# A third buffer in SBUF for the decays and states of a selective scan, and the shared bias as two rows of a low-rank product

## The chip, the cores and the metric

The kernel runs on one core of one Trainium2 chip. The metric is the device time of one execution in microseconds (us). TensorE is PE in the rows, VectorE is DVE, ScalarE is ACT, GpSimd is POOL, SyncE is SP.

## The reference, cut to what matters

The input is one sequence of 4096 tokens with 512 channels, float32. A layer norm is followed by a selective scan with 16 states per channel, its output is normed and added; then comes a mixture of 8 experts (top 2, 2048 hidden units, a low-rank side path of rank 32) and a shared expert that every token passes:

```python
dt = softplus(x_low @ W_dt + b_dt); A = -exp(A_log)
h  = exp(dt * A) * h + (dt * x) * B_t          # one state of 16, for every channel
y  = sum_n(h_n * C_t[n]) + x * D_skip
...
sh = gelu(xt @ sw1 + sb1) @ sw2 + sb2
sh = sh + gelu(xt @ swd) @ swu
out = out + 0.2 * sh
```

## The kernel before, in words

There are three stages, one after the other: `prepare` (norm, projections, step sizes), `mix` (the recurrence, with the shared expert of the first 7 of 8 blocks of 512 tokens laid between), and `experts` (the last shared block and the experts). The change is in `mix`.

`mix` walks over units g = 0 to 511, then on to 575 without a recurrence. A unit is one state n (16) of one group of 128 channels (4) of one chunk of 512 tokens (8), so 64 units make a chunk. Each engine has its own loop over g, and its instructions run in that written order; semaphores tie the engines together. For unit g:

- GpSimd (`drive`, L897) multiplies `dtx` by the row of B into `u`, a ring of 6, up to 5 units ahead. It may write `u` of unit g only when the scan of unit g - 6 is done. Both inputs lie in SBUF.
- ScalarE (`decay`, L646) writes exp(dt * A) into a buffer `bank(g)`. Before that it copies the last column of the unit that had the buffer (`keep`, L635) and so waits for that unit's product.
- VectorE (`recur`, L790) scans in place: bank = bank * previous + u. Then (`weigh`, L797) it multiplies bank by the row of C into `pr`, a ring of 5.
- TensorE (`add`, L1014) adds `pr` into PSUM by four transposing matmuls.

PSUM has eight banks. The shared expert needs four for its sums (`psS`), one for `psH`, and `psY` takes one, so `bank(g)` has two PSUM banks (`psA`). Up to unit 116 (`WIDE` = 117) the first `psS` bank is still free and serves as a third. With three, VectorE is told to do scan g + 1 and then product g; with two, it does scan g and product g in turn, and ScalarE is two units ahead instead of three.

The shared expert of block b sits at hand-written unit numbers from the start of chunk b + 1: `UP_AT` the first products (L1050), `BURST_AT` the gelus on ScalarE, `HI_AT` and `LO_AT` the split of the hidden values in a high and a low part (L715 on ScalarE, L906 on GpSimd, which reads SBUF only), `DOWN_AT` the second products (L1061, L1071). GpSimd also issues the loads of its weights (L950, L959), each when a slot is free. At unit 119 of a block (`OUT_AT`) VectorE takes the four `psS` banks out, times 0.2 plus the bias 0.2 * sb2 that a 128 x 512 tile `b2bc` holds (`shared_out`, L841). `low_rank_lo` (L828) forms the low part of the low-rank hidden values, from two SBUF tiles into one. `static_lo` (L847 to L853) prepares the low-rank weights once, at unit 10.

## Time and profile before

| what | value |
|---|---|
| median of 3 runs | 3389.76 us (3389.55 to 3391.35) |
| span of the profiled execution, first to last instruction | 3388.4 us |
| `prepare` in the trace | 0 to about 150 us |
| units 0 to 116, three buffers | about 152 to 393 us |
| units 117 to 511, two buffers | about 393 to 1306 us |
| rest of the last shared block | 1306 to about 1387 us |
| `experts` | about 1387 us to the end |

No time is given for the profiled execution apart from its span; the span is 1.4 us short of the median of the runs, which is what lies around it. Times in the trace count from the first instruction. "Busy" is the time in which an engine carries out an instruction; idle time stands beside it with what ended it.

### The profile page before, as it was taken

How to read it: one execution, taken by the hardware profiler on the slowest of the kernel's cores; microseconds unless marked ns; L12 is line 12 of the kernel's file. 1: busy time of each engine (PE TensorE's matmuls, PEld its weight loads, DVE VectorE, ACT ScalarE, POOL GpSimd, SP SyncE). 2: the span in 40 equal slices, each digit the busy share in tenths (PEclk: the TensorE clock that was granted, in tenths of full speed). 3: DMA queues.
4: the chain of work that ended last, by engine and by line, in shares of the span. 5: the costliest groups of instructions: out<-in, count | busy, mean ns of one | idle time of the engine just before them, and what ended most of it. 6: DMA issues, size and time to landing. Idle time of an engine off the chain costs nothing.

```text
span 3388.4 us, 42962 instructions
## 1 busy us (share of the span) xinstructions
PE 3100.0 (91%) x15139; PEld 2538.6 (75%) x15139; DVE 1812.1 (53%) x2476; ACT 1633.6 (48%) x2978; POOL 1384.2 (41%) x1367
## 2 busy tenths in 40 slices
PE   6464799988989899999999999999999999999997
PEld 3243677777767777788888888888888888888886
DVE  7797989988998984441331332322313313313345
ACT  7654676666767665452332432433423424324343
POOL 2297787988988785311110121021111111211224
PEclk9655899999999999999999999999999999999999
DMA  7968678696977865930320420412312303204355
GB/s 265 303 189 250 163 229 217 203 268 183 257 192 225 230 190 186 288 95 19 88 69 13 106 60 16 119 37 54 97 20 75 78 16 100 63 10 115 75 184 161
DMA packets 273447, 466.30 MB, mean 138 GB/s; under 512 B 30817, under 2 KB 102193, under 8 KB 273234
## 3 DMA queue, kind: packets, MB, share of 16 engines
q1 hardware_dynamic: 200400, 264.91, 26.5%
q0 software_dynamic: 66720, 189.87, 21.3%
q10 hardware_dynamic: 6114, 8.79, 0.7%
q8 instruction: 121, 1.98, 0.2%
q14 instruction: 92, 0.75, 0.1%
HBM read 366.33 MB, written 97.16 MB: 137 GB/s over the span
## 4 chain that ended last, share of the span: by engine, by line
PE 53%; DMA 2%; DVE 2%; issue 1%; ACT 1%; POOL 0%; SPq 0%; POOLq 0%; DVEq 0%; ACTq 0%
PE c_psH L2030 26%; PE c_psY L2071 25%; PE c_psT L2021 1%; DMA out<-d_y 1%; PE c_psY L2067 0%; DVE yst L1734 0%; DMA raw<-in_w 0%; DMA W2l<-ws_d 0%; DVE hl L1754 0%; ACT h L1487 0%; DVE hl L1759 0%; DVE wgt L1923 0%; PE c_psT L2130 0%; DVE hh L1753 0%; DMA d_x1p<-x_d 0%
## 5 line engine op out<-in xcount | busy, mean ns | idle before, releaser
L1759 DVE TENSOR_TENSOR hl<-h,hh 128x512 fp32r<-128x512 f32 (+1 forms) x400 | 242.5, 606 | 1185.3 <-ACT hh L1491 1185.2
L1489 ACT ACTIVATE h<-c_psH,biases 128x512 f32<-128x512 f32 (+1 forms) x400 | 248.1, 620 | 1045.0 <-PE c_psH L2030 1033.0
L897 POOL TENSOR_TENSOR u<-dtxs,Bt 128x512 f32<-128x512 f32 x512 | 669.3, 1348 | 148.2 <-DVE b_psA L790 132.9
L790 DVE TENSOR_TENSOR_SCAN b_psA<-b_psA,b_few,u 128x512 f32<-128x512 f32 x473 | 606.4, 1282 | 75.0 <-ACT b_psA L646 74.0
L2071 PE MATMUL c_psY<-W2h,hh 128*128 128x512 f32 x1344 | 535.2, 398 | 1.8 <-DVE hl L1759 1.1
L1014 PE MATMUL b_psY<-ident,pr 128*128 128x128 f32 x2048 | 345.7, 308 | 208.2 <-DVE pr L797 190.1
L2071 PE MATMUL c_psY<-W2l,hh 128*128 128x512 f32 x1344 | 525.4, 391 | 0.0
L2071 PE MATMUL c_psY<-W2h,hl 128*128 128x512 f32 x1344 | 524.4, 390 | 0.0
L1567 POOL DMA_INDIRECT xrow<-xt_d,slot_lists x80 | 84.7, 1059 | 1050.3 <-PE c_psT L2021 600.2
L1014 PEld LDWEIGHTS b_psY<-ident,pr 128*128 128x128 f32 x2048 | 265.9, 156 | 290.8 <-DVE pr L797 238.7
L646 ACT ACTIVATE b_psA<-dts,wgt 128x512 f32<-128x512 f32 x473 | 327.4, 692 | 14.9 <-ACT b_few L635 0.2
L797 DVE TENSOR_TENSOR pr<-b_psA,Ct 128x512 f32<-128x512 f32 x473 | 325.5, 688 | 14.4 <-DMA Ct<-bc_d 0.7
L1050 PE MATMUL b_psH<-Xh,w 128*128 128x512 f32 x896 | 316.7, 415 | 9.9 <-DMA w<-ws_d 9.7
L1607 POOL DMA_INDIRECT acc_d<-yst,slot_lists x72 | 117.4, 1630 | 442.7 <-DVE yst L1734 425.3
L2071 PEld LDWEIGHTS c_psY<-W2h,hl 128*128 128x128 f32 x1344 | 252.8, 188 | 54.9
L2071 PEld LDWEIGHTS c_psY<-W2h,hh 128*128 128x128 f32 x1344 | 253.2, 188 | 53.2 <-DVE hl L1759 6.2
L1071 PE MATMUL b_psS<-w,hhs 128*128 128x512 f32 x896 | 292.7, 408 | 0.0
L2071 PEld LDWEIGHTS c_psY<-W2l,hh 128*128 128x128 f32 x1344 | 253.5, 189 | 46.6 <-issue 0.2
L1491 ACT ACTIVATE hh<-c_psH,biases 128x512 fp32r<-128x512 f32 (+1 forms) x400 | 245.1, 613 | 0.0
L2030 PE MATMUL c_psH<-Xh,W1h 128*128 128x512 f32 x576 | 224.5, 390 | 0.7 <-DMA W2l<-ws_d 0.7
L2030 PE MATMUL c_psH<-Xl,W1h 128*128 128x512 f32 x576 | 224.3, 389 | 0.0
L2030 PE MATMUL c_psH<-Xh,W1l 128*128 128x512 f32 x576 | 224.2, 389 | 0.0
(271 smaller groups left out, 5685.1 us busy)
## 6 DMA issues: line engine op xcount, KB each, us to landing
w<-ws_d POOLq DMA_DIRECT2D x224, 512.0 KB, 6.6
raw<-in_w SPq DMA_DIRECT2D x256, 256.0 KB, 2.8
Bt<-bc_d SPq DMA_DIRECT2D x64, 512.0 KB, 14.6
Ct<-bc_d SPq DMA_DIRECT2D x64, 512.0 KB, 19.1
xn<-in_x SPq DMA_DIRECT2D x8, 1024.0 KB, 7.9
xT_d<-xnT SPq DMA_DIRECT2D x8, 1024.0 KB, 12.5
dt_d<-a_dt SPq DMA_DIRECT2D x8, 1024.0 KB, 8.5
dtx_d<-a_dx SPq DMA_DIRECT2D x8, 1024.0 KB, 8.7
```

What stands on the lines that cost most here:

```text
L646: nc.scalar.activation(bank(g)[:, :], dts[s % 2][:, :], ACT.Exp, scale=A_neg[:, s % DT, n:n + 1]).then_inc(s_dA, 1)
L790: nc.vector.tensor_tensor_scan(a[:, :], a[:, :], u[g % U_RING][:, :], carry[:, k:k + 1], ALU.mult, ALU.add).then_inc(s_h, 1)
L797: nc.vector.tensor_tensor(pr[g % PR_RING][:, :], bank(g)[:, :], C_of(g), ALU.mult)\
L897: nc.gpsimd.tensor_tensor(u[g % U_RING][:, :], dtx[s % 2][:, :], Bt[n // TG][:, n % TG, :], ALU.mult)\
L1014: last = nc.tensor.matmul(psY[:, t, :], pr[g % PR_RING][:, t * P:(t + 1) * P], ident[:, :], start=(n == 0 and t == 0), stop=False, is_tran ...
L1050: last = nc.tensor.matmul(out, a[:, d, :], v[:, d, :], start=(d == 0 and i == 0), stop=(d == DT - 1 and i == 2))
L1071: last = nc.tensor.matmul(psS[t][:, :], a, v, start=False, stop=(j == FC and i == 2))
L1489: nc.scalar.activation(h32[:, 0:n * P], psH[j % 2][:, 0:n * P], ACT.Gelu, bias=b1[:, j - 1:j])
L1491: nc.scalar.activation(hh[j % 2][:, 0:n * P], psH[j % 2][:, 0:n * P], ACT.Gelu, bias=b1[:, j - 1:j]).then_inc(s_gelu, 1)
L1759: nc.vector.tensor_tensor(hl[j % 2][a], h32[a], hh[j % 2][a].bitcast(F32), ALU.subtract)\
L2030: last = nc.tensor.matmul(out, a, b, start=(i == 0), stop=(i == n - 1))
L2071: last = nc.tensor.matmul(psY[t][:, :], a[j % 2][:, c], b, start=False, stop=(j == J - 1 and i == 2))
```

## The change: what it does, and the diff

From unit 117 on, every third unit (g % 3 = 2) uses `decay_aside`, a 128 x 512 tile in SBUF, as its `bank`; the others use the two `psA` banks in turn. So there are three buffers throughout, ScalarE is three units ahead in all units, and VectorE does scan g + 1 before product g in all units. Units 0 to 116 keep their three PSUM banks.

The tile `b2bc` and its load go. `sb2` comes as two rows below the low-rank weights `L2`, which grow from 96 to 98 rows; the rows hold the high and the low part of sb2, and `hh0` gets two rows of ones against them. `static_lo` makes these rows by three more VectorE instructions of 2 x 512. `shared_out` becomes a plain multiplication by 0.2 on ScalarE, one bank at each of units 119 to 122.

```diff
-        g0, hh0 = sb("g0", [P, CH]), sb("b_low_h", [L3, CH], F32R)
-        b2bc = sb("sb2bc", [P, D])
+        aside = sb("decay_aside", [P, CH])
+        g0, hh0 = sb("g0", [P, CH]), sb("b_low_h", [L3B, CH], F32R)
         yst = two("ysh", [P, D]) + xn
...
         def bank(g):
 
-            if g < WIDE:
-                return (psA + psS[0:1])[g % 3]
-            return psA[(g - WIDE) % 2]
+            if g % 3 < 2:
+                return psA[g % 3]
+            return psS[0] if g < WIDE else aside
...
                 sp.dma_start(wu_raw[k * LR:(k + 1) * LR, :], w["swu"]).then_inc(s_stat, 16)
+            sp.dma_start(wu_raw[L3:L3B, :], w["sb2"].partition_broadcast(2)).then_inc(s_stat, 16)
             for i in range(4):
                 load_raw(i)
-            sp.dma_start(b2bc[:, :], w["sb2"].partition_broadcast(P)).then_inc(s_bias, 16)
...
                     for t in range(BT):
-                        if due(b, OUT_AT) + 1 + t == g:
+                        if due(b, OUT_AT + t) + 1 == g:
                             store_sh(b, t)
...
             def decay(g):
-                s, n, old = g // NS, g % NS, g - (3 if g < WIDE + 2 else 2)
+                s, n, old = g // NS, g % NS, g - 3
                 if n == 0:
                     loaded(act, s)
-                if g == WIDE + 2:
-                    keep(old - 1)
                 if old >= 0:
                     keep(old)
                     act.wait_ge(s_cd, old + 1)
...
-                nc.scalar.copy(hh0[:, :], g0[0:L3, :]).then_inc(s_h0a, 1)
+                nc.scalar.copy(hh0[0:L3, :], g0[0:L3, :]).then_inc(s_h0a, 1)
...
+            def shared_out(b, t):
+                if b < FB - 1:
+                    act.wait_ge(s_mm2, (b + 1) * J)
+                else:
+                    act.wait_ge(s_tile, t + 1)
+                after(act, s_sh[t], b * 16)
+                if t >= 2:
+                    act.wait_ge(s_T, min(b + 2, FB + 1) * BT)
+                    act.wait_ge(s_xt[t - 2], min(b + 2, FB + 1) * (BT // 2) * 16)
+                nc.scalar.mul(yst[t][:, :], psS[t][:, :], SHARE).then_inc(s_yev, 1)
...
-                if g + 3 < WIDE + 2:
+                if g + 3 < UNITS:
                     decay(g + 3)
-                elif WIDE + 2 <= g + 2 < UNITS:
-                    decay(g + 2)
                 if g == 6:
                     static_hi()
-                if g == NU:
-                    act.wait_ge(s_bias, 32)
-                    nc.scalar.mul(b2bc[:, :], b2bc[:, :], SHARE).then_inc(s_b02, 1)
...
+                    for t in range(BT):
+                        if due(b, OUT_AT + t) == g:
+                            shared_out(b, t)
...
+            nc.vector.memset(hh0[L3:L3B, :].bitcast(F32), 1.0).then_inc(s_one, 1)
...
-            def shared_out(b, t):
-                if b < FB - 1:
-                    dve.wait_ge(s_mm2, (b + 1) * J)
-                else:
-                    dve.wait_ge(s_tile, t + 1)
-                dve.wait_ge(s_b02, 1)
-                after(dve, s_sh[t], b * 16)
-                if t >= 2:
-                    dve.wait_ge(s_T, min(b + 2, FB + 1) * BT)
-                    dve.wait_ge(s_xt[t - 2], min(b + 2, FB + 1) * (BT // 2) * 16)
-                nc.vector.scalar_tensor_tensor(yst[t][:, :], psS[t][:, :], SHARE, b2bc[:, :], ALU.mult, ALU.add)\
-                    .then_inc(s_yev, 1)
-
             def static_lo():
-                dve.wait_ge(s_stat, 5 * 16)
+                dve.wait_ge(s_stat, 6 * 16)
...
+                two_rows = slice(L3, L3B)
+                nc.vector.tensor_tensor(bias_low, wu_raw[two_rows, :], L2[two_rows, :].bitcast(F32),
+                                        ALU.subtract).then_inc(s_blow, 1)
+                dve.wait_ge(s_blow, 1)
+                nc.vector.tensor_scalar(bias_low, bias_low, ident[two_rows, L3 + 1:L3 + 2], None, ALU.mult)\
+                    .then_inc(s_blow, 1)
+                dve.wait_ge(s_blow, 2)
+                nc.vector.scalar_tensor_tensor(L2[two_rows, :], L2[two_rows, :].bitcast(F32), ident[two_rows, L3:L3 + 1],
+                                               bias_low, ALU.mult, ALU.add).then_inc(s_l2, 1)
...
-                if g <= WIDE:
-                    if g == 0:
-                        recur(0)
+                if g == 0:
+                    recur(0)
+                if g + 1 < UNITS:
                     recur(g + 1)
-                    weigh(g)
-                elif g < UNITS:
-                    if g > WIDE + 1:
-                        recur(g)
+                if g < UNITS:
                     weigh(g)
 
...
+                    pe.wait_ge(s_one, 1)
                     for t in range(BT):
-                        last = nc.tensor.matmul(psS[t][:, :], hh0[:, t * P:(t + 1) * P], L2[:, :], start=True, stop=False)
+                        last = nc.tensor.matmul(psS[t][:, :], hh0[0:L3B, t * P:(t + 1) * P], L2[0:L3B, :],
+                                                start=True, stop=False)
                 else:
```

## Rows read from the trace of the kernel before

**Rows 1.** Chain that ended last, share of the span, by engine.

```profile
PE 53%; DMA 2%; DVE 2%; issue 1%; ACT 1%; POOL 0%; SPq 0%; POOLq 0%; DVEq 0%; ACTq 0%
```

**Rows 2.** Busy time in stretches: length, engines' busy us (instructions), clock, DMA share, GB/s.

```profile
393.00:1306.00 913.00, 818.57 (x4329) 677.03 (x4328) 822.93 (x943) 618.56 (x1155) 763.96 (x746) 0.96 0.77 217
1306.00:1387.00 81.00, 76.66 (x347) 62.30 (x345) 11.66 (x25) 28.32 (x36) 37.65 (x65) 0.98 0.64 200
1387.00:3388.40 2001.40, 1975.89 (x9625) 1654.45 (x9625) 650.00 (x1141) 746.79 (x1397) 353.09 (x359) 1.00 0.30 80
```

**Rows 3.** VectorE's groups by line, 393 to 1306 us: busy, mean ns | idle before.

```profile
L790 DVE TENSOR_TENSOR_SCAN b_psA<-b_psA,b_few,u 128x512 f32<-128x512 f32 x395 | 506.9, 1283 | 54.8 <-ACT b_psA L646 53.8 <-POOL u L897 0.5
L797 DVE TENSOR_TENSOR pr<-b_psA,Ct 128x512 f32<-128x512 f32 x396 | 273.9, 692 | 13.6
L822 DVE TENSOR_TENSOR Xl<-b_psH,Xh 128x512 fp32r<-128x512 f32 x24 | 16.5, 686 | 17.0 <-ACT Xh L676 17.0
L812 DVE BATCH_NORM_STATS2 b_few<-ys 128x6 f32<-128x512 f32 x24 | 15.2, 682 | 3.5 <-DMA ys<-in_x 3.5
L802 DVE BATCH_NORM_STATS2 b_few<-ys 128x6 f32<-128x512 f32 x24 | 14.8, 680 | 0.1
L828 DVE TENSOR_TENSOR b_low_h<-g,b_low_h 32x512 fp32r<-32x512 f32 x7 | 8.1, 1154 | 0.2
L841 DVE SCALAR_TENSOR_TENSOR ysh<-b_psS,sb2bc 128x512 f32<-128x512 f32 x12 | 7.7, 681 | 0.0
```

**Rows 4.** VectorE's timeline in the two-buffer stretch: start us, length us, what.

```profile
801.46 1.28 DVE L790 TENSOR_TENSOR_SCAN b_psA<-b_psA,b_few,u 128x512 f32<-128x512 f32 x1
802.78 0.69 DVE L797 TENSOR_TENSOR pr<-b_psA,Ct 128x512 f32<-128x512 f32 x1
803.38 1.28 DVE L790 TENSOR_TENSOR_SCAN b_psA<-b_psA,b_few,u 128x512 f32<-128x512 f32 x1
```

**Rows 5.** VectorE's timeline in the three-buffer stretch.

```profile
167.90 1.28 DVE L790 TENSOR_TENSOR_SCAN b_psS<-b_psS,b_few,u 128x512 f32<-128x512 f32 x1
169.09 0.67 DVE L797 TENSOR_TENSOR pr<-b_psA,Ct 128x512 f32<-128x512 f32 x1
169.68 1.28 DVE L790 TENSOR_TENSOR_SCAN b_psA<-b_psA,b_few,u 128x512 f32<-128x512 f32 x1
```

**Rows 6.** ScalarE's groups by line, 393 to 1306 us.

```profile
L646 ACT ACTIVATE b_psA<-dts,wgt 128x512 f32<-128x512 f32 x394 | 272.8, 692 | 12.3
L635 ACT COPY b_few<-b_psA 128x1 f32<-128x1 f32 x394 | 61.2, 155 | 177.1 <-DVE pr L797 173.8
L676 ACT CAST Xh<-b_psH 128x512 fp32r<-128x512 f32 x24 | 14.0, 584 | 7.7 <-PE b_psH L1033 7.7
```

**Rows 7.** VectorE's groups by shape, whole span: instructions with only SBUF operands.

```profile
L1756 DVE TENSOR_TENSOR hh<-h,hl 32x512 fp32r<-32x512 f32 x17 | 11.6, 683 | 0.6
...
L853 DVE TENSOR_TENSOR L<-ys,L 32x512 fp32r<-32x512 f32 x1 | 1.7, 1685 | 0.0
...
L1830 DVE TENSOR_TENSOR_SCAN RA<-xrow,RB 128x512 f32<-128x512 f32 x1 | 1.2, 1225 | 0.0
```

**Rows 8.** VectorE's timeline around the last low-rank split.

```profile
1291.48 1.28 DVE L790 TENSOR_TENSOR_SCAN b_psA<-b_psA,b_few,u 128x512 f32<-128x512 f32 x1
...
1293.53 1.16 DVE L828 TENSOR_TENSOR b_low_h<-g,b_low_h 32x512 fp32r<-32x512 f32 x1
```

**Rows 9.** GpSimd's timeline over the same time.

```profile
1292.85 1.29 POOL L897 TENSOR_TENSOR u<-dtxs,Bt 128x512 f32<-128x512 f32 x1 [0.64 <-DVE b_psA L790]
1294.10 1.72 POOL L906 TENSOR_TENSOR hls<-hb,hhs 128x512 fp32r<-128x512 f32 x1
```

**Rows 10.** GpSimd's groups by line, 393 to 1306 us.

```profile
L897 POOL TENSOR_TENSOR u<-dtxs,Bt 128x512 f32<-128x512 f32 x390 | 514.0, 1351 | 135.2 <-DVE b_psA L790 124.0 <-DMA dtxs<-dtx_d 2.9 <-DVE b_psS L790 0.4
L906 POOL TENSOR_TENSOR hls<-hb,hhs 128x512 fp32r<-128x512 f32 x100 | 134.5, 1345 | 1.1 <-ACT hhs L715 1.0
...
L959 POOL DMA_DIRECT2D w<-ws_d x96 | 65.4, 681 | 0.0
```

More of the change, by code:

```diff
@@ L367 @@
 L3 = 3 * LR
+L3B = L3 + 2
 T_AT, X_HI_AT, X_LO_AT = (24, 27, 31, 34), (25, 29, 32, 35), (27, 31, 34, 37)
@@ L447, in mix @@
         s_sh = [sem(f"b_sh_stored{t}") for t in range(BT)]
-        s_bias, s_b02 = sem("b_biases_in"), sem("b_bias_scaled")
+        s_bias, s_blow, s_one = sem("b_biases_in"), sem("b_bias_low"), sem("b_bias_rows_of_ones")
         s_wr = [sem(f"b_raw_w_in{k}") for k in range(4)]
@@ L456, in mix @@
         gate_raw = ys[1][:, 1, 0:DT * E].rearrange("p (a n) -> p a n", a=DT)
-        wu_raw = ys[1][0:L3, 2, :]
+        wu_raw = ys[1][0:L3B, 2, :]
+        bias_low = ys[1][L3:L3B, 3, :]
         def raw_pair(i):
@@ L689, in hidden_out @@
                     act.wait_ge(s_wl, FC)
-                    act.wait_ge(s_bias, 32)
+                    act.wait_ge(s_bias, 16)
                 nc.scalar.activation(hb[:, n % HB_RING, :], psH[:, :], ACT.Identity,
@@ L731, in static_hi @@
             def static_hi():
-                act.wait_ge(s_stat, 5 * 16)
+                act.wait_ge(s_stat, 6 * 16)
                 nc.scalar.copy(L1h[:, :, 0:L3].rearrange("p a (g n) -> p a g n", g=3),
@@ L864, in _ @@
                 for b in blocks(g):
-                    if due(b, OUT_AT) == g:
-                        for t in range(BT):
-                            shared_out(b, t)
                     if due(b, LOW_LO_AT) == g:
@@ L1039, in up @@
                     pe.wait_ge(s_llo, 2)
-                    pe.wait_ge(s_l2, 1)
+                    pe.wait_ge(s_l2, 2)
                     wh, wl = L1h, L1l
@@ L1308, in piece @@
                 a = slice((w_ - 2) * 256, (w_ - 1) * 256)
-                return WU[:, a], r[0:L3, 0:256], L2[:, a], L2[0:LR, a], r[0:L3, 0:256]
+                return WU[:, a], r[0:L3, 0:256], L2[0:L3, a], L2[0:LR, a], r[0:L3, 0:256]
             j = (w_ - 4) // 2
@@ L2066, in down @@
                                 pe.wait_ge(s_yev, at["t0"] - (2 if at["k"] == 1 else 4) + min(t, 1 if at["k"] == 1 else 3) + 1)
-                            last = nc.tensor.matmul(psY[t][:, :], hh[0][0:L3, c], L2[:, :], start=True, stop=False)
+                            last = nc.tensor.matmul(psY[t][:, :], hh[0][0:L3, c], L2[0:L3, :], start=True, stop=False)
                             continue
@@ L2215, in program @@
             kept_tile("edge2", [P, 8], F32)
-            const["L2"] = kept_tile("L2", [L3, D])
+            const["L2"] = kept_tile("L2", [L3B, D])
             const["X"] = [kept_tile(f"X{h}", [P, DT, CH]) for h in "hl"]
```

1 line of the change is left out of this document (removed).

## The prediction

> **What bounds the kernel now.** I read the chain first, for where a saving could count [rows 1]: TensorE holds 53% of it, VectorE 2%. That sum is over stages with different limits, so I cut the span into stages [rows 2]. From 1306 us on TensorE is busy 95 to 99% of the time, and the change touches nothing there but the four last reads of PSUM. What it touches is the stretch of units 117 to 511, 913 us long. There TensorE is busy 818.6 us and VectorE 822.9 us, and GpSimd 764.0 us. The next view says what VectorE does with its time [rows 3]: 395 scans and products, and beside them the parts of the shared expert, the statistics, and the waits in front.
>
> The pace of a unit comes from the timeline. With two buffers scan follows scan after 803.38 - 801.46 = 1.92 us [rows 4]; with three, where the next scan stands between a scan and its product, after 169.68 - 167.90 = 1.78 us [rows 5]. The difference is that the product starts 1.32 us after its scan in the one and 1.19 us after the scan before it in the other.
>
> The 913 us of VectorE then add up: 395 x 1.92 = 758; waits for ScalarE's decays 54; the split of X 16.5 + 17.0 of wait; statistics 15.2 + 3.5 + 14.8 and about 5 of their short second halves, in smaller groups; low-rank split 8; taking out the shared sums 24 x 0.64 = 15 (12 of them stand in the row, 12 more cost the same) [rows 3]. That is 908, so VectorE's queue sets the pace here, the product of each unit feeds TensorE, and what is left of TensorE's time, 913 - 819 = 94 us, is the room below it. When the recurrence is over, 81 us of TensorE work remain whatever came before [rows 2]: a shift of the recurrence shifts the end by the same amount, as long as TensorE is not itself the bound.
>
> **What the change takes away.** (a) The pace: 395 x (1.92 - 1.78) = 55 us. (b) The waits for decays, 53.8 us [rows 3]. They come when ScalarE's gelus stand ahead of a decay. ScalarE will be three units ahead instead of two, one unit more is 1.78 us, and ScalarE waited 174 us for products over the stretch [rows 6], so it has the time. I let 10 us stay: -44. (c) `shared_out` leaves VectorE: -15. On ScalarE it costs 24 x 0.58 = 14 us by the copy of a bank of the same size [rows 6], in the same 174 us of waiting; without that cover it would come back as 14 us of decays. In the ScalarE queue the decay of three units ahead stands behind each of the four, at one per unit, and the last second product is due 7 units ahead of them, so no new wait for TensorE is likely. At the end of the last block four takings on one engine replace four on the other: 0. The scaling of `b2bc` and its load go, off the path: 0. Two more rows in four matmuls a block cost 0, since the rows are contracted in parallel, and their columns stay.
>
> VectorE's sum without anything else would be 913 - 55 - 44 - 15 = 799 us, and TensorE's 819 would stop it first.
>
> **What the change adds: operands in SBUF on an engine that shares.** Units 119 to 509 in steps of 3 are 131. Their scan reads `aside` and `u`, both in SBUF; their product reads `aside` and the row of C, both in SBUF. Before, one operand was always in PSUM. Alone this costs nothing: a scan of this size with SBUF operands took 1225 ns and a 512-wide product 683 ns, both with GpSimd idle [rows 7]; the decay's write to SBUF instead of PSUM I put at 0, inside ScalarE's slack.
>
> With GpSimd at work it is another matter. `low_rank_lo` is the one repeated instruction of this stage with two SBUF inputs, and it takes 1154 ns [rows 3] where the same shape takes 683 in the last stage [rows 7]. Its neighbours show why. It starts at 1293.53 while GpSimd's `u` runs until 1292.85 + 1.29 = 1294.14, and it ends at 1294.69, 0.55 us behind that [rows 8, 9]. GpSimd's next instruction starts at 1294.10 and takes 1.72 us instead of 1.29, so it ends at 1295.82, 1.13 us behind VectorE's end: it too waited. Each works only when the other has finished. Once-run L853 was 1685 ns in the same way [rows 7]. The product is delayed here by 0.47 us, GpSimd by 0.44 us (1.72 - 1.28). No scan with two SBUF inputs next to a busy GpSimd is in the trace. I take it to behave as this product does, bounded below by 0 (no collision) and above by a whole GpSimd instruction, 1.29 us.
>
> On VectorE: `u` starts 0.09 us after the end of the scan that frees it (1291.48 + 1.28 = 1292.76, then 1292.85) [rows 8, 9]. It ends 1.38 us after that scan. The next scan comes 1.78 - 1.28 = 0.50 us after it, so a scan into `aside` waits 0.88 us, less the 0.14 that a waiting instruction has saved of its start (0.69 - 0.55): 0.74 us. The product into `pr` comes 1.19 us after the start of the scan ahead of it, before that scan's end has released `u`; it waits nothing where GpSimd is caught up, and about 0.47 where GpSimd is in arrears. I take 0.25. That gives 131 x 0.74 = 97 and 131 x 0.25 = 33, and VectorE's sum is 799 + 130 = 929 us.
>
> On GpSimd: a product holds it up 0.44 us; a scan takes 0.53 us longer to stream (1225 against 683 ns), so 0.97. Where GpSimd is only issuing DMAs it reads nothing; the share of its time in `u` and the low parts is (514.0 + 134.5) / 764 = 85% [rows 2, 10]. Its sum is 764 + 131 x 1.41 x 0.85 = 921 us.
>
> So two engines that had slack toward each other come to 929 and 921, and GpSimd's work is uneven. Between units 59 and 105 of a block stand 16 low parts, 16 weight loads of one kind and about 14 of the other: (16 x 1.25 + 30 x 0.68) / 46 x 3 = 2.6 us per three units, with 3 x 1.25 for `u` and 1.2 for the collisions 7.6 us, or 2.5 us a unit; VectorE's own is 929 / 395 = 2.35. With 46 of 64 units at 2.5 and 18 at 2.35 the stretch would be 971 us. The five units that GpSimd may be ahead smooth part of that. I take the middle of 929 and 971: 950 us, +37 us.
>
> The Trainium skill, SBUF — State Buffer, section "Who interferes with whom", states that a VectorE instruction with two SBUF inputs and a GpSimd instruction that reads SBUF exclude each other for the whole instruction, whoever came first. With whole instructions (1.28 + 0.69) in place of the trace's 1.41 GpSimd's sum would be 764 + 131 x 1.97 x 0.85 = 983 us instead of 921; the trace agrees with the exclusion and not quite with its length, since 0.44 us was lost for a 0.69 us instruction.
>
> (d) Three more VectorE instructions in `static_lo`, in the early stretch where its queue is tight: two with two SBUF inputs like L853, at most 1.69 each [rows 7], one with a single input, about 0.5, each behind a wait on the one before: between 2 and 4, I take +4 us.
>
> Sum: +37 + 4 = +41 us. Against the profiled span 3388.4 that is 3429.4; the median of the runs lies 1.4 above the span: 3431 us.
>
> **The rivals.** *It gets faster: scans don't collide.* The trace shows the collision for products only. If a scan in SBUF runs beside GpSimd, VectorE comes to 799 + 33 = 832 and GpSimd to 764 + 131 x 0.44 x 0.85 = 813, TensorE's 819 is next to them, and with as much unevenness as above (+21) the stretch takes about 853: 3390 - 60 + 4 = 3334 us. The place is the 131 scans alone; it turns at the price per scan at which VectorE's sum plus 21 is 913, (913 - 853) / 131 = 0.46 us. For it speaks that a scan takes 1.28 us for 512 columns, over twice a product's streaming, so it asks for operands at half the rate; against it, that what was seen was no sharing of a rate but a wait until the other had ended.
>
> *It gets much slower: the arrears chain.* A low part that comes late holds TensorE's second product, which stands in the same queue as the sums of `pr`; the ring of 5 fills, and ScalarE's next split waits for TensorE. Then every product waits 0.47, VectorE's sum is 799 + 131 x 1.21 = 958, and the two kinds of wait for ScalarE (54 + 17, of which 10 + 17 were kept) come back with 44, to 1002: 3390 + 89 + 4 = 3483 us. For it speaks that ScalarE and TensorE already wait on one another here; against it, the 94 us of room in TensorE.
>
> *It does nothing.* Gains of 114 us (55 + 44 + 15) against 114 us of collisions: that needs 0.87 us per unit into `aside`, between the two prices above, 3390 us. Nothing favours this point, it only lies on the way.
>
> **How the numbers follow.** My forecast's case (both collide, 3395 to 3465) 0.50; the chain (above 3465) 0.17; the faster case (below 3383) 0.26, some of it with part of the collision; within the band of no change 0.07. A measurement of this kernel tells a change from none at about 0.2%, 7 us. The range goes from 3334 to 3485, the rival's time on either side; a tenth may lie beyond each end. The likeliest case alone: 3402 (products free, no unevenness beyond GpSimd's 921) to 3465.
>
> **What would show it.** In the changed profile the scans into `aside` should last 1.8 to 2.2 us instead of 1.28 and their products up to 1.2; GpSimd's `u` should have a longer mean than 1351 ns and wait less for scans than 124 us; the waits of L790 for ScalarE should fall from 54 to about 10; scans into `psA` should keep their 1.28. The stretch from unit 117 to 511 should take 950 us. Scans into `aside` at 1.23 to 1.3 us would make the forecast wrong and the faster rival right. TensorE waiting for low parts (L906), which it does not now, would point to the chain.

## The result, and the profile after

| | before | after |
|---|---|---|
| median of 4 runs each on one chip | 3390.56 us | 3518.50 us (3516.77 to 3523.50) |
| span of the profiled execution | 3388.4 us | 3516.7 us |
| units 117 to 511 | 393 to 1306 us, 913 us | 393 to 1434 us, 1041 us |
| what remains of the last shared block | 81 us | 82 us |

The ratio is 1.0377 (1.0365 to 1.0390): 128 us slower. The direction was forecast (3431 us), the size was not: 3518 lies above the end of the range, 3485. All of the difference is in the stretch of units 117 to 511, 1041 - 913 = 128 us, where 950 us stood in the forecast. That is read from the stretches of the kernel after (columns as in [rows 2]):

```profile
393.00:1434.00 1041.00, 855.49 (x4350) 691.99 (x4349) 1000.51 (x924) 640.45 (x1185) 825.89 (x751) 0.94 0.69 192
1434.00:1516.00 82.00, 77.76 (x352) 63.14 (x350) 8.57 (x20) 31.47 (x43) 38.52 (x67) 0.98 0.65 202
```

VectorE was busy 822.9 us there before [rows 2] and is busy 1000.5 of 1041 us now: it is the bound, with hardly a gap. GpSimd, which the forecast had at 921 us, is at 826. VectorE's groups over that stretch, kernel after (busy us, mean ns | idle before), against [rows 3]:

```profile
L800 DVE TENSOR_TENSOR_SCAN b_psA<-b_psA,b_few,u 128x512 f32<-128x512 f32 x266 | 339.5, 1276 | 17.9 <-ACT b_psA L646 17.6
L800 DVE TENSOR_TENSOR_SCAN decay_aside<-decay_aside,b_few,u 128x512 f32<-128x512 f32 x131 | 286.4, 2186 | 12.9 <-ACT decay_aside L646 11.0 <-ACT b_few L637 1.8
L807 DVE TENSOR_TENSOR pr<-decay_aside,Ct 128x512 f32<-128x512 f32 x131 | 199.7, 1524 | 0.1
L807 DVE TENSOR_TENSOR pr<-b_psA,Ct 128x512 f32<-128x512 f32 x266 | 176.5, 664 | 0.1
L832 DVE TENSOR_TENSOR Xl<-b_psH,Xh 128x512 fp32r<-128x512 f32 x24 | 16.3, 677 | 6.3 <-ACT Xh L676 6.3
```

Two kinds of row stand next to each other here, one in PSUM and one in SBUF, and only the second has changed. Scans into `psA` keep their 1276 ns; scans into `decay_aside` take 2186, so 131 x 0.910 = 119 us more. Products from `psA` take 664 ns; those from `decay_aside` take 1524, so 131 x 0.860 = 113 us more. These are 232 us in place of the 130 forecast. Waits for decays are 17.6 + 11.0 + 1.8 = 30.4 us (53.8 before, 10 forecast). With 397 x 1.78 = 707 us for the units, 22.6 for the split of X, about 35 for the statistics and 10 for the low-rank split the sum is 707 + 232 + 30 + 23 + 35 + 10 = 1037 of 1041 us. The rows account for the whole stretch.

The means hide how the collisions are distributed. The tile's own view of the kernel after gives shortest, median and longest, in ns:

```profile
L800 DVE TENSOR_TENSOR_SCAN decay_aside<-decay_aside,b_few,u x131: 1253/1943/4872, 401.2 to 1425.9; 128x512 f32<-128x512 f32 x131
L807 DVE TENSOR_TENSOR pr<-decay_aside,Ct x131: 662/674/5229, 407.6 to 1428.9; 128x512 f32<-128x512 f32 x131
```

Half of the products pass unhindered (674 ns), and yet their mean is 1524: the sum is in a tail of up to 5.2 us, four times a GpSimd instruction. Over all 131 units, 30 products and 27 scans lost more than 1.3 us each, a whole GpSimd instruction; these 57 waits hold 151 of the 232 us (about 91 in the products and 60 in the scans). The other 101 products lost 0.22 us on average, the other 104 scans 0.57. One of the long waits in VectorE's timeline, kernel after, with the three added instructions of `static_lo` above it:

```profile
177.39 1.64 DVE L853 TENSOR_TENSOR ys<-ys,L 2x512 f32<-2x512 f32 x1
179.07 0.48 DVE L856 TENSOR_SCALAR ys<-ys,ident 2x512 f32<-2x512 f32 x1
179.59 0.75 DVE L859 SCALAR_TENSOR_TENSOR L<-L,ident,ys 2x512 fp32r<-2x512 f32 x1
...
802.69 1.28 DVE L800 TENSOR_TENSOR_SCAN b_psA<-b_psA,b_few,u 128x512 f32<-128x512 f32 x1
803.88 4.83 DVE L807 TENSOR_TENSOR pr<-decay_aside,Ct 128x512 f32<-128x512 f32 x1
808.64 1.28 DVE L800 TENSOR_TENSOR_SCAN b_psA<-b_psA,b_few,u 128x512 f32<-128x512 f32 x1
```

And GpSimd over the same time, kernel after:

```profile
803.20 0.58 POOL L950 DMA_DIRECT2D w<-ws_d  x1
803.79 1.31 POOL L897 TENSOR_TENSOR u<-dtxs,Bt 128x512 f32<-128x512 f32 x1
805.06 1.29 POOL L906 TENSOR_TENSOR hls<-hb,hhs 128x512 fp32r<-128x512 f32 x1
806.29 0.57 POOL L959 DMA_DIRECT2D w<-ws_d  x1
806.88 1.27 POOL L897 TENSOR_TENSOR u<-dtxs,Bt 128x512 f32<-128x512 f32 x1
```

The product should have waited for the `u` of 803.79 and then had its turn. It waited through three reading instructions and a DMA issue, and ended at 803.88 + 4.83 = 808.71, 0.56 us behind the end of the last (806.88 + 1.27 = 808.15). GpSimd's instructions meanwhile kept their 1.3 us: it did not give way once. 0.56 us is what a product had left to run in [rows 8, 9] too (0.55), so the end of a wait looked as forecast, and its length did not.

### The profile page after: what moved, and what is told of

The parts are those of the page before. It is cut to its first block, busy times and chain, and to the rows that moved or that the text cites. A ratio compares the mean times of both kernels' runs of the same rounds, so it can differ in the third digit from the quotient of the medians.

```text
span 3516.7 us, 42960 instructions
## 1 busy us (share of the span) xinstructions
PE 3134.1 (89%) x15139; PEld 2550.1 (73%) x15139; DVE 1985.6 (56%) x2452; ACT 1654.3 (47%) x3004; POOL 1443.0 (41%) x1367
## 4 chain that ended last, share of the span: by engine, by line
PE 51%; DVE 2%; DMA 2%; issue 1%; ACT 1%; SPq 0%; POOL 0%; POOLq 0%; DVEq 0%; ACTq 0%
PE c_psH L2032 25%; PE c_psY L2073 24%; PE c_psT L2023 1%; DMA out<-d_y 1%; DMA raw<-in_w 1%; PE c_psY L2069 0%; DVE yst L1736 0%; DVE hl L1756 0%; ACT h L1489 0%; DVE hl L1761 0%; PE c_psT L2132 0%; DVE hh L1755 0%; DMA d_x1p<-x_d 0%; DVE wgt L1925 0%; ACT h L1491 0%
## 5 line engine op out<-in xcount | busy, mean ns | idle before, releaser
L897 POOL TENSOR_TENSOR u<-dtxs,Bt 128x512 f32<-128x512 f32 x512 | 698.1, 1387 | 178.8 <-DVE b_psA L800 86.0
L1014 PE MATMUL b_psY<-ident,pr 128*128 128x128 f32 x2048 | 361.1, 312 | 312.9 <-DVE pr L807 287.7
L800 DVE TENSOR_TENSOR_SCAN b_psA<-b_psA,b_few,u 128x512 f32<-128x512 f32 x342 | 436.4, 1276 | 36.4 <-ACT b_psA L646 36.0
L1073 PE MATMUL b_psS<-w,hhs 128*128 128x512 f32 x896 | 303.4, 421 | 0.0
L800 DVE TENSOR_TENSOR_SCAN decay_aside<-decay_aside,b_few,u 128x512 f32<-128x512 f32 x131 | 286.4, 2186 | 12.9 <-ACT decay_aside L646 11.0
L646 ACT ACTIVATE b_psA<-dts,wgt 128x512 f32<-128x512 f32 x342 | 236.6, 692 | 10.9 <-ACT b_few L637 0.2
L807 DVE TENSOR_TENSOR pr<-b_psA,Ct 128x512 f32<-128x512 f32 x342 | 227.5, 665 | 0.6 <-DMA Ct<-bc_d 0.5
```

The source lines that it names most:

```text
L646: nc.scalar.activation(bank(g)[:, :], dts[s % 2][:, :], ACT.Exp, scale=A_neg[:, s % DT, n:n + 1]).then_inc(s_dA, 1)
L800: nc.vector.tensor_tensor_scan(a[:, :], a[:, :], u[g % U_RING][:, :], carry[:, k:k + 1], ALU.mult, ALU.add).then_inc(s_h, 1)
L807: nc.vector.tensor_tensor(pr[g % PR_RING][:, :], bank(g)[:, :], C_of(g), ALU.mult)\
L897: nc.gpsimd.tensor_tensor(u[g % U_RING][:, :], dtx[s % 2][:, :], Bt[n // TG][:, n % TG, :], ALU.mult)\
L1014: last = nc.tensor.matmul(psY[:, t, :], pr[g % PR_RING][:, t * P:(t + 1) * P], ident[:, :], start=(n == 0 and t == 0), stop=False, is_tran ...
L1073: last = nc.tensor.matmul(psS[t][:, :], a, v, start=False, stop=(j == FC and i == 2))
```

## The experiments

Times of the kernel before in the comparisons were 3390 to 3397 us; each ratio is against those of its own chip.

**The bias alone.** `shared_out` on ScalarE and the bias as rows, with the buffers and the order of the kernel before.

```diff
+TWO = 117
...
+            if g >= TWO:
+                return psA[(g - TWO) % 2]
```

> The bias as two rows and the taking out of the shared sums on ScalarE are kept; the buffers and the order of units are those of before (two PSUM banks from unit 117 on). If the whole loss comes from operands in SBUF, this part is a small gain: 24 takings x 0.64 = 15 us off VectorE, about 3 us lost in the static part: 3373 to 3380 us. If the takings on ScalarE delay decays and are part of the loss, it is slower than before: 3395 us or more.

3391.35 us, ratio 1.0005 (0.9994 to 1.0015): no change. The 15 us that left VectorE came back in front of its scans. The scans' row over 397 to 1316 us, kernel with the bias alone, against the 53.8 of [rows 3]:

```profile
L807 DVE TENSOR_TENSOR_SCAN b_psA<-b_psA,b_few,u 128x512 f32<-128x512 f32 x395 | 507.0, 1283 | 72.4 <-ACT b_psA L651 70.9 <-POOL u L907 1.0
```

**The SBUF buffer in half of the units.** `decay_aside` for units 117 to 314 (66 of them), two buffers after that, by the same edit with `TWO = 315` and the order of scans and products to match.

> The changed kernel with the SBUF buffer for units 117 to 314 alone (66 of its 131 units), two PSUM banks after that. If each unit in SBUF pays for itself, the time lies halfway between the bias part alone and the full change: about 3446 us. If the loss is an engine that falls into arrears over the whole stretch, the first half costs less than the second and the time is below 3420 us.

Ratio 1.0189 (1.0166 to 1.0211), some 3453 us, half of the way. The scans into `decay_aside` took 2146 ns and their products 1547, as in the whole. So the loss goes with the number of SBUF units, and the bias contributes nothing of its own. The order of scans and products changed together with the buffer, so this run does not tell the two apart.

**Turns by force.** GpSimd's `u` waits until the scan and the product of the SBUF unit are done, so that it can't run ahead of them.

```diff
+                if g - 5 > WIDE and (g - 5) % 3 == 2:
+                    pool.wait_ge(s_h, g - 5 + 1)
+                if g - 6 > WIDE and (g - 6) % 3 == 2:
+                    pool.wait_ge(s_pd, g - 6 + 1)
```

> The changed kernel with two more waits on GpSimd: around each unit in SBUF the next u starts only when that unit's scan is done, and the one after only when its product is done. GpSimd does the same work, with fewer chances to run on ahead. If VectorE's two-input instructions lose because GpSimd chains several instructions before it lets them in, this is faster than the changed kernel: 3430 to 3480 us. If GpSimd's own sum is what bounds the changed kernel, added waits on it make it slower: 3530 us or more.

3491.47 us, ratio 1.0301 (1.0282 to 1.0319): 27 us of the 128 came back. The products fell from 1524 to 1222 ns, the scans rose from 2186 to 2318. The time lies between the two that were expected. It helped part of the products, and gave no cause.

**The collision by itself.** A kernel that computes nothing of the reference: GpSimd runs a chain of six 128 x 512 products from SBUF, VectorE starts beside it a delay with an operand in PSUM and then one instruction under test.

> No part of the reference is computed. Twenty short cases one after the other: GpSimd runs six products of 128 x 512 from SBUF, without or with a wait that is already met before each, and VectorE issues one product or one scan at different offsets, with both inputs in SBUF, one in PSUM, or on 32 partitions. If the two take turns, VectorE's instruction lasts at most about 1.9 us (the rest of one GpSimd instruction and its own 0.55), a scan 2.4. If GpSimd keeps the port while it has work, VectorE's lasts to the end of the six: 5 to 7 us. With one input in PSUM 0.69 us in any case; alone 0.69 and 1.23.

VectorE's timeline of this kernel; L104 is the delay, L107 the product with one operand in PSUM, L109 the product with two in SBUF, L113 the scan with two in SBUF:

```profile
15.90 0.68 DVE L107 TENSOR_TENSOR do<-ps,db 128x512 f32<-128x512 f32 x1
23.07 0.43 DVE L104 TENSOR_TENSOR pre<-ps,da 128x256 f32<-128x256 f32 x1 [6.48 <-ACTq L86]
23.41 0.68 DVE L109 TENSOR_TENSOR do<-da,db 128x512 f32<-128x512 f32 x1
24.16 0.42 DVE L104 TENSOR_TENSOR pre<-ps,da 128x256 f32<-128x256 f32 x1
24.50 1.27 DVE L113 TENSOR_TENSOR_SCAN do<-da,few,db 128x512 f32<-128x512 f32 x1
25.85 0.23 DVE L104 TENSOR_TENSOR pre<-ps,da 128x64 f32<-128x64 f32 x1
25.99 1.72 DVE L109 TENSOR_TENSOR do<-da,db 128x512 f32<-128x512 f32 x1
...
66.00 2.04 DVE L113 TENSOR_TENSOR_SCAN do<-da,few,db 128x512 f32<-128x512 f32 x1
...
122.89 10.05 DVE L109 TENSOR_TENSOR do<-da,db 128x512 f32<-128x512 f32 x6
```

Beside GpSimd the product in PSUM takes its 0.68 us; with two operands in SBUF it is 0.68 without GpSimd and up to 1.72 with it, and a scan goes from 1.27 to 2.04: scans do collide, which ended the faster rival. But even six products in a row took turns with GpSimd, 10.05 us for six, 1.68 each. No wait here was longer than one GpSimd instruction. That left the tail without a cause.

**GpSimd that doesn't read.** From unit 117 on `u` is filled with a constant and not computed, in the kernel after and in the kernel before.

```diff
+                if g < WIDE:
                     nc.gpsimd.tensor_tensor(u[g % U_RING][:, :], dtx[s % 2][:, :], Bt[n // TG][:, n % TG, :], ALU.mult)\
                         .then_inc(s_u, 1)
+                else:
+                    nc.gpsimd.memset(u[g % U_RING][:, :], 0.5).then_inc(s_u, 1)
```

> The changed kernel, but from unit 117 on GpSimd fills u with a constant instead of multiplying two SBUF tiles into it: the product dt*x*B is left out there. GpSimd then reads SBUF only for the low parts (100 instructions in the stretch). If VectorE's two-input instructions wait for GpSimd's reads, scans into the SBUF buffer fall from 2.19 to about 1.4 us and their products from 1.52 to about 0.8, and the time falls to 3320 to 3360 us. If operands in SBUF are slow in themselves, or any GpSimd instruction collides, the scans stay near 2 us and the time above 3450 us.

> The kernel before with the same constant fill in place of dt*x*B from unit 117 on, as the measure for the run above. GpSimd does not set the pace there, so 3380 to 3392 us. If this one falls to 3350 us or less, GpSimd was part of the bound before the change, and my reading of that stretch was wrong.

The kernel after: 3377.26 us, ratio 0.9955 (0.9939 to 0.9971). The kernel before: 3381.31 us, 0.9970 (0.9959 to 0.9980). VectorE's groups, 397 to 1292 us, kernel after with the fill:

```profile
L800 DVE TENSOR_TENSOR_SCAN b_psA<-b_psA,b_few,u 128x512 f32<-128x512 f32 x264 | 338.0, 1280 | 59.7 <-ACT b_psA L646 59.2
L800 DVE TENSOR_TENSOR_SCAN decay_aside<-decay_aside,b_few,u 128x512 f32<-128x512 f32 x131 | 176.2, 1345 | 20.7 <-ACT decay_aside L646 19.7 <-ACT b_few L637 0.9
L807 DVE TENSOR_TENSOR pr<-b_psA,Ct 128x512 f32<-128x512 f32 x263 | 175.4, 667 | 0.1
L807 DVE TENSOR_TENSOR pr<-decay_aside,Ct 128x512 f32<-128x512 f32 x131 | 106.6, 814 | 0.1
```

Two things are seen. The scans are back at 1345 ns and the products at 814. A fill is also shorter than a product (549 ns on average), so the means alone could come from a GpSimd that has less to do. The single instructions settle it: of the 262 on the SBUF buffer 133 ran beside fills and not beside a reading instruction, and none of them was delayed; all 28 that were delayed by more than 0.1 us stood beside an instruction that reads. So the collision is with GpSimd's reads: it cost 3518 - 3377 = 141 us between these two kernels. The Trainium skill, SBUF — State Buffer, section "Who interferes with whom", states that a VectorE instruction with two SBUF inputs contends with a GpSimd instruction that reads SBUF and not with one that only writes it; 1345 against 2186 ns agrees. And without the collision the change is worth 3381 - 3377 = 4 us, hardly more than the runs scatter, not the 114 of the forecast: 59.2 + 19.7 = 79 us of waits for decays stand where 10 were expected.

**Where the 114 us went.** The same pair, with the third of the three products of each high and low pair left out (`up` and `down` with two instead of three), so that TensorE has less work.

```diff
-                    for i, (a, v) in enumerate(((wh, Xh), (wh, Xl), (wl, Xh))):
+                    for i, (a, v) in enumerate(((wh, Xh), (wh, Xl))):
...
-                        for i, (a, v) in enumerate(((hi, w2h), (hi, w2l), (lo, w2h))):
+                        for i, (a, v) in enumerate(((hi, w2h), (hi, w2l))):
```

> The changed kernel with the constant fill of u, and TensorE's work for the shared expert made lighter: of three products per pair of high and low parts the third is left out (L1050 and its sister), in the scan stage. Without collisions the change was worth only 4 us of 114. If that is because TensorE's queue, with ScalarE waiting behind it, bounds the stretch, this kernel falls well below 3377 us, to 3290 to 3330 us, and its VectorE waits 20 us or less for decays. If ScalarE's gelus alone hold the decays up, it stays above 3350 us.

> The kernel before with the same fill and the same lighter TensorE, the measure for the run above. VectorE's pace of 1.92 us a unit and its waits for gelus bound it then: 3350 to 3370 us, 30 us or more above its sister. If both fall together, the third buffer is worth nothing in any case.

After 3324.05 us, 0.9806 (0.9777 to 0.9834); before 3338.68 us, 0.9849 (0.9820 to 0.9877). The change is now worth 15 us instead of 4, less than expected. Lighter TensorE work took 53 us off the one and 43 off the other, so TensorE was part of the floor, and not all of it: 59 us of waits for decays stay, where 20 or less were expected. Waits for transfers come up as well: in the kernel after so lightened TensorE waits 23 us for weights (0.4 with the fill alone) and ScalarE 25 us for step sizes (3.6), over 393 to 1292 us. In the kernel after with the fill, ScalarE was then freed of its gelu tables by an identity in the gelu's place.

```diff
-                    nc.scalar.activation(hb[:, k:k + 2, :], hb[:, k:k + 2, :], ACT.Gelu).then_inc(s_g, 1)
+                    nc.scalar.activation(hb[:, k:k + 2, :], hb[:, k:k + 2, :], ACT.Identity).then_inc(s_g, 1)
```

> The changed kernel with the constant fill of u, and the gelus of the scan stage replaced by the identity, on the same engine: their values are left out, and with them the loads of the function tables, 50 x 1.28 us. If ScalarE's bursts are what keeps VectorE waiting, 3300 to 3335 us; if it is TensorE, not below 3355 us.

3351.28 us, 0.9886 (0.9857 to 0.9915): 26 us less, short of the 3335 us that were expected of ScalarE alone. Not all of it need be ScalarE's, since the granted clock of TensorE over 397 to 1240 us was 0.99 here and 0.96 with the fill alone. ScalarE and TensorE each seem to hold a part; how large each is stays open. In the trace of the kernel after with the fill, over the same 397 to 1292 us, ScalarE waits 66.7 us for TensorE's first products, and TensorE 73.4 us for VectorE's: the three wait in a ring, and shortening one of them moves the others little.

**Relative starts.** The collision by itself again, in 30 cases: a scan ahead of the product, a product ahead of the scan, and delays of 64 to 512 columns.

> No part of the reference is computed. GpSimd runs six products of 128 x 512 from SBUF in a row; VectorE issues one instruction with two SBUF inputs, in 15 steps of about 33 ns against GpSimd's chain: a product behind a scan from PSUM and ahead of another, and a scan between two products from PSUM, as in the changed kernel. If what VectorE runs ahead decides whether it gets its turn, some offsets show a product of 2.5 us and more (two or more GpSimd instructions passed). If they always take turns, all lie between 0.67 and 1.9 us (scans 1.25 to 2.4), and what lets GpSimd pass several times in the kernel is something else.

Products 1.28 to 1.74 us, scans 1.27 to 1.65. No start gave a wait beyond one GpSimd instruction.

**The SBUF buffer only where the gelus stand.** 25 units in place of 131: one ahead of each of the four bursts of a block, the rest on two PSUM banks.

```diff
+        in_sbuf = {(b + 1) * NU + at + 3 for b in range(FB) for at in BURSTS if (b + 1) * NU + at + 3 > WIDE}
...
+            return (psA + psS[0:1] + [aside])[keys[g]]
```

> The SBUF buffer is used for 25 units alone, each the third unit after the start of a burst of gelus on ScalarE, so that one more decay is ready there; all others use two PSUM banks, and the bias part is kept. Against the bias part alone (3391 us) it should take back most of VectorE's 70 us of waits for decays, -50, and pay 25 times the collisions that the changed kernel paid per unit (0.91 + 0.86 us), +44, less the pace of the units behind it, 50 x 0.14 = 7: 3370 to 3390 us. If a unit in SBUF costs more at these places, because GpSimd has its low parts to do right behind the bursts, 3400 us or more.

3423.71 us, ratio 1.0089 (1.0072 to 1.0106), so 32 us lost by 25 units, where 3370 to 3390 us had been expected. That is a miss, and it pointed to the cause. The tile's view and VectorE's timeline of this kernel:

```profile
L817 DVE TENSOR_TENSOR_SCAN decay_aside<-decay_aside,b_few,u x25: 1257/1260/10183, 400.5 to 1319.7; 128x512 f32<-128x512 f32 x25
```

```profile
764.41 8.72 DVE L817 TENSOR_TENSOR_SCAN decay_aside<-decay_aside,b_few,u 128x512 f32<-128x512 f32 x1 [0.78 <-ACT decay_aside L661]
```

GpSimd in the same time:

```profile
764.30 0.59 POOL L979 DMA_DIRECT2D w<-ws_d  x1
764.90 2.56 POOL L917 TENSOR_TENSOR u<-dtxs,Bt 128x512 f32<-128x512 f32 x2
767.40 1.30 POOL L926 TENSOR_TENSOR hls<-hb,hhs 128x512 fp32r<-128x512 f32 x1
768.64 0.58 POOL L970 DMA_DIRECT2D w<-ws_d  x1
769.23 1.27 POOL L917 TENSOR_TENSOR u<-dtxs,Bt 128x512 f32<-128x512 f32 x1
770.46 1.26 POOL L926 TENSOR_TENSOR hls<-hb,hhs 128x512 fp32r<-128x512 f32 x1
771.67 0.58 POOL L979 DMA_DIRECT2D w<-ws_d  x1
```

One scan of 8.72 us let five reading instructions pass, and it had asked just when a weight load was being issued (764.30); the product of 803.88 above had asked right behind such an issue (803.20). The trace of the kernel after says the same when its delayed scans and products are sorted by what GpSimd was at when they asked, with more of its work to follow without a gap:

| GpSimd at the request | delayed | passed by a further reading instruction |
|---|---|---|
| at a DMA issue, or right behind one | 57 | 50 |
| an issue two or four instructions back | 31 | 7 |
| no issue since GpSimd's last gap | 56 | 0 |

In 30 of the 31 an instruction of an SBUF unit had been served since the issue. In a few cases it is open whether they belong in the first row or the second.

The table holds delayed requests alone, and that hides half of the first row. 42 requests fell into an issue itself, while GpSimd read nothing. 27 of them went at once, 15 were delayed, and 13 of these let a reading instruction pass. Of the 39 that fell into the first reading instruction behind an issue, or came as it started, with more behind it, every one was delayed and 35 let a further one pass. So an issue does not always shut VectorE out; what the 27 had in their favour is not known.

How the waits ended can be read too. The 57 that let a further reading instruction pass ended 34 times with GpSimd's queue empty and 23 times while GpSimd was at a later DMA issue, never with a reading instruction directly behind. The product of 540.56 us took 3.00 us in this way: it let two `u` pass and had its turn when the issue of 542.95 began.

**Other suspects.** The collision by itself in 28 cases: semaphore waits on VectorE, waits on GpSimd, a scan in place, and a DMA issue after the second product of the chain, which is later than VectorE's request.

> No part of the reference is computed. Seven kinds of case at four offsets each, with GpSimd running six products from SBUF: a plain product behind a scan from PSUM; with met waits in front of it; with a DMA issue in GpSimd's chain; a scan in place; waits on both sides; GpSimd waiting for VectorE's semaphore; and all together. If one of these lets GpSimd pass several times, that kind shows a VectorE instruction of 2.5 us and more. If none does, all products stay below 1.9 and scans below 2.4 us, and the cause lies in something of the full kernel that these leave out.

Products 1.28 to 1.75 us, scans 1.81 to 2.27. All took turns; waits and the in-place form are not the cause, and neither is an issue that comes after the request.

**The weight loads issued elsewhere.** The loads of L950 and L959, 112 of each, in the kernel after and in the kernel before are issued by SyncE, with the same waits and the same places in the order of units (the tile is taken as plain float32 there). The 192 of the two expectations is too low: in units 117 to 511 of the kernel after stand 198 of the 224:

```profile
L950 POOL DMA_DIRECT2D w<-ws_d x101 | 64.4, 638 | 12.3 <-PE b_psH L1050 10.9 <-issue 1.4
L959 POOL DMA_DIRECT2D w<-ws_d x97 | 64.3, 663 | 3.6 <-PE b_psS L1073 3.2 <-issue 0.4
```

```diff
-                nc.gpsimd.dma_start(w1[k][:, :, :, :].rearrange("p h a f -> p (h a f)"),
+                sp.dma_start(w1[k][:, :, :, :].rearrange("p h a f -> p (h a f)").bitcast(F32),
```

> The changed kernel with the 192 loads of the shared expert's weights issued by SyncE at the same unit numbers instead of GpSimd. GpSimd's queue gets shorter by 129 us of issues in the stretch and its products stand less often in arrears. If VectorE's long waits (2.5 us and more) come of a GpSimd that has several instructions due at once, they get fewer and the time falls by 30 to 60 us, to 3460 to 3490 us. If a DMA issue in GpSimd's chain is itself what shuts VectorE out, they vanish altogether and it falls by 80 us or more. If neither, 3510 to 3525 us.

> The kernel before with the same loads issued by SyncE, the measure for the run above. GpSimd had slack there, so the loads alone should change nothing: 3385 to 3395 us. If SyncE's queue holds the loads behind its other waits, TensorE waits for weights and it is slower.

After 3446.49 us, 1.0163 (1.0146 to 1.0180); before 3435.77 us, 1.0129 (1.0112 to 1.0146). VectorE's groups, 393 to 1434 us, kernel after with the loads on SyncE:

```profile
L829 DVE TENSOR_TENSOR_SCAN decay_aside<-decay_aside,b_few,u 128x512 f32<-128x512 f32 x131 | 238.7, 1822 | 21.9 <-ACT decay_aside L675 20.8 <-ACT b_few L666 0.8
...
L836 DVE TENSOR_TENSOR pr<-decay_aside,Ct 128x512 f32<-128x512 f32 x131 | 147.6, 1127 | 0.1
```

The waits over 1.3 us fall from 57 to 8, and what they hold from 151 to 28 us. GpSimd still issues the loads of `x` (L951, 16 of them), and all 8 long waits asked at or behind one of these.

A rival is left: without the issues GpSimd might simply have less in arrears, so that less stands ready to pass. The trace says no. 113 delayed requests met a GpSimd that had more to follow without a gap and had issued nothing since its last gap, twice the 56 of the kernel after, and none was passed by a further instruction.

The change now costs 3446 - 3436 = 11 us and not 128. The 11 us is not the price of the short collisions: scans and products on the SBUF buffer still take 71 + 61 = 132 us more than as many in PSUM (1822 against 1278 ns, 1127 against 665), and the kernel before lost 46 us by the move. SyncE is no gain by itself: TensorE waits 45.0 us for weights in the kernel before with the loads there (9.7 without the move), and VectorE 98.2 us for decays (53.8).

**The issue ahead of the request.** The collision by itself in 28 cases, with one DMA issue ahead of the first, second or third of GpSimd's six products, and VectorE's request after 1, 3, 5 or 7 delays of 0.6 us.

```diff
+                    if what != "none" and j == at:
+                        nc.gpsimd.dma_start(px[:, :], a["x"][0:P, :]).then_inc(s_x, 16)
                     nc.gpsimd.tensor_tensor(po[j][:, :], pa[:, :], pb[:, :], ALU.mult).then_inc(s_p, 1)
```

> No part of the reference is computed. In the changed kernel 50 of 57 requests of VectorE that met a GpSimd instruction directly behind a DMA issue, or the issue itself, with more of GpSimd's work behind, were passed by at least one more; of 93 others 7 were. So here GpSimd runs six products from SBUF with one DMA issue ahead of the first, second or third, and VectorE asks with two SBUF inputs after 1, 3, 5 or 7 delays of 0.6 us. If the issue is the cause, requests that come behind it last to the end of the chain, 3 us and more; requests ahead of it and the cases without an issue at most 1.9 us. If the link in the kernel is by chance of timing, none lasts over 1.9. With a memset (1 or 256 columns) between the issue and the products, the long ones go away if any instruction in between ends it.

VectorE's timeline of this kernel, L99 the delays (the first rows without an issue, those from 48.94 with one ahead of the first product, those from 84.46 with one ahead of the second):

```profile
25.05 1.89 DVE L99 TENSOR_TENSOR pre<-ps,da 128x512 f32<-128x512 f32 x3 [6.10 <-ACTq L75]
26.85 1.28 DVE L100 TENSOR_TENSOR do<-da,db 128x512 f32<-128x512 f32 x1
...
49.55 8.30 DVE L100 TENSOR_TENSOR do<-da,db 128x512 f32<-128x512 f32 x1
57.92 1.89 DVE L99 TENSOR_TENSOR pre<-ps,da 128x512 f32<-128x512 f32 x3
59.73 6.97 DVE L100 TENSOR_TENSOR do<-da,db 128x512 f32<-128x512 f32 x1
...
85.07 1.25 DVE L100 TENSOR_TENSOR do<-da,db 128x512 f32<-128x512 f32 x1
92.54 1.89 DVE L99 TENSOR_TENSOR pre<-ps,da 128x512 f32<-128x512 f32 x3 [6.22 <-ACTq L75]
94.34 6.74 DVE L100 TENSOR_TENSOR do<-da,db 128x512 f32<-128x512 f32 x1
```

GpSimd, the same kernel:

```profile
85.71 0.58 POOL L83 DMA_DIRECT2D px<-in_x  x1
...
93.79 0.58 POOL L83 DMA_DIRECT2D px<-in_x  x1
94.39 6.13 POOL L92 TENSOR_TENSOR po<-pa,pb 128x512 f32<-128x512 f32 x5
```

The request of 85.07 came before the issue of 85.71 and had its turn: 1.25 us. That of 94.34 came behind the issue of 93.79 and ended at 101.08, 0.56 us after the end of GpSimd's whole chain (94.39 + 6.13 = 100.52). All 28 cases follow that line; requests ahead of the issue, and those without one, wait for one GpSimd instruction:

| issue | after 1 delay | 3 | 5 | 7 |
|---|---|---|---|---|
| none | 1.25 | 1.28 | 1.30 | 1.33 |
| ahead of product 1 | 8.30 | 6.97 | 5.78 | 4.58 |
| ahead of product 2 | 1.25 | 6.74 | 5.54 | 4.36 |
| ahead of product 3 | 1.25 | 1.28 | 5.55 | 4.35 |
| ahead of 1, then a fill of 1 column | 8.19 | 7.01 | 5.80 | 4.62 |
| ahead of 3, then a fill of 1 column | 1.25 | 1.28 | 5.59 | 4.39 |
| ahead of 2, then a fill of 256 columns | 1.25 | 6.98 | 5.79 | 4.60 |

**A small fill behind each issue.** The kernel after, with a one-column fill behind each of GpSimd's issues of weights and of `x` (240 fills of 196 ns in the trace, not the 208 of the expectation).

> The changed kernel with a memset of one column on GpSimd behind each of its 208 DMA issues. If an instruction between the issue and the next reading one gives VectorE its turn back, the 57 long waits (151 us) shrink to one GpSimd instruction each (about 45 us): 3518 - 100 = 3420 us, 3400 to 3460. If the memset changes nothing but GpSimd's load (208 x 0.15 = 31 us), 3518 to 3540 us.

3517.65 us, 1.0355 (1.0338 to 1.0372), scans 2286 and products 1422 ns: no help, as the last lines of the table say; 58 waits are over 1.3 us.

No version tried beats the kernel before with the reference's computation; the bias alone equals it.

## Why the prediction was right in direction and wrong in size

**The failed step** is the length of a wait: "it waits nothing where GpSimd is caught up, and about 0.47 where GpSimd is in arrears. I take 0.25", and for the scan the upper bound "a whole GpSimd instruction, 1.29 us". The product's term was 131 x 0.25 = 33 us and measured 113; that is 80 of the 91 us missing from the stretch. The assumption under it was taken from one neighbouring pair [rows 8, 9]: each waits for one instruction of the other. It holds as long as GpSimd has issued no DMA. In the isolated cases a VectorE instruction with two SBUF inputs that asks after an issue lets every reading instruction of GpSimd's queue pass: 8.30 us against 1.25. In the kernel after it lets, beside the one that runs, one to three further ones pass (up to 5.2 us), until the queue is empty or GpSimd issues again. GpSimd issues its weight loads in this stretch [rows 10], 198 of them in the kernel after and in the middle of its low parts, where its queue doesn't run empty. The move of the loads to SyncE (57 long waits to 8) shows that it is what happens here. Without the long waits the products lost 0.22 us on average: the 0.25 was right for what it described.

**The scan's term**, 131 x 0.74 = 97 us, measured 119. Outside the long waits it is 0.57 us, in them 2.2 (59.8 / 27). That it collides at all was the open question of the forecast, and it was answered as forecast.

**Decay waits**: 10 us forecast, 30.4 measured, so 20 more. **X waits**: 17 kept, 6.3 measured, 11 less. **Unevenness**: 21 us were added for GpSimd's uneven work; it was not needed, since GpSimd, busy 826 us and waiting 160.8 us in front of `u`, did not become the bound. From 950: 950 - 21 + 22 + 80 + 20 - 11 = 1040 us, against 1041.

**The decay's write to SBUF**, put at 0, took 723 ns against 692: 131 x 0.03 = 4 us on ScalarE, which waited 357 us for products there.

**GpSimd's cost** was forecast at +157 us (764 to 921) and measured +62 (826). It is held up when VectorE comes first; the long waits are those in which it isn't.

**The gains (a), (b), (c)** are where the forecast was wrong without its showing. In VectorE's own rows (a) is there: 397 units at 1.78 us. But 55 + 44 + 15 = 114 us off VectorE's queue shorten nothing by 114. The bias alone gave 0 for its 15, its decay waits rising by 17; with the fill, the three together gave 4 us. The forecast's floor was TensorE's 819 us plus 21. The one seen is 1292 - 393 = 899 us for the kernel after with the fill, in which VectorE waits 79 us for decays, ScalarE 66.7 for TensorE and TensorE 73.4 for VectorE. The faster rival, 3334 us, would therefore not have come even with hardly a collision (3377 us with the fill). The slower rival, the arrears chain, gave 3483 and so lay near the time, for another reason: TensorE did not wait for low parts, and the waits for ScalarE fell.

**The static part** took 1.64 + 0.48 + 0.75 and its gaps, 180.37 - 177.39 = 3.0 us; 4 were forecast. The 81 us behind the recurrence stayed (82).

## What to carry to other kernels

Before an operand of a VectorE instruction moves from PSUM to SBUF, look at what GpSimd does beside it: here a second SBUF input cost up to one GpSimd instruction (1.3 us) where GpSimd only computed, and several of them (2.2 to 10.2 us in all) where GpSimd had just issued a DMA. Read minimum, median and longest of a tile, not only the mean; a product with a median of 674 ns and a mean of 1524 has a second mechanism in its tail. And a sum over one engine's queue tells what more work on it costs, but not what less work brings, when its neighbours wait for each other with ten per cent of slack: a kernel in which the disputed collision is taken away prices the gain by itself.

## What the runs showed of the hardware

Two SBUF inputs make a VectorE product or scan collide with a GpSimd instruction that reads SBUF (0.68 to 1.72 us, 1.27 to 2.04) and hardly with one that only fills (814 and 1345 ns as means in the kernel). Without a DMA issue the two take turns, also over six in a row (10.05 us). After GpSimd has issued a DMA they don't, in the isolated cases without exception: a product that asks later ends 0.56 us after GpSimd's chain (4.35 to 8.30 us), and a fill of 1 or 256 columns behind the issue doesn't restore the turns. The Trainium skill, SBUF — State Buffer, section "Who interferes with whom", lets whoever issues first keep the shared pair for that instruction; 1.25 us agrees with it, 8.30 us doesn't, and the measurement decides. What ends this state is known in part. In the isolated cases it was always the end of GpSimd's queue. In the kernel after, 34 of 57 such waits ended so and 23 at a later DMA issue, and the 8.72 us scan above also had its turn about when GpSimd was at a third issue (771.67), since it ended at 773.13 and a scan of the kernel after ended about 1.1 us behind the end of its wait. But other issues were passed over, that of 806.29 for one, and which issue ends a wait stays open. So does why 27 of 42 requests that came during an issue went at once, and why turns were mostly back (24 of 30) once one VectorE instruction had been served, which no isolated case tried. Why an issue has this effect was not found out, nor whether the DMA must be a load, as all of these were.
